# Attention and a quantized MLP on one core: the two score products as pairs of 64-row matmuls, with a ring of three PSUM banks

## The reference

```
x = x + attention(layernorm(x))       # 16 heads of 16 columns
    xw  = x_h @ w_att_val[h]
    att = softmax(xw @ x_h.T / 4)     # [512, 512] per head and batch
    o   = att @ (x @ wv_w.T + wv_b)_h
    attention = o @ out_w.T + out_b
x = x + ffn(layernorm(x))             # blockwise 4-bit quantization, silu(gate) * up, down
```

## Time and profile before

| | |
|---|---|
| median of three runs (lowest, highest) | 1645.03 us (1640.6, 1647.64) |
| profiled execution, first to last instruction | 1643.6 us |
| what the median has beyond that span | 1.4 us |
| attention, about | 66 us to 1075 us |
| MLP | the rest, to 1643.6 us |
| PE busy, DVE busy, ACT busy, POOL busy | 96%, 85%, 51%, 20% |

### The profile page before, as it was taken

One profiled execution on the slowest core, in us unless ns is written; L12 is line 12 of the kernel. 1 busy time (PEld: TensorE's weight loads), 2 busy tenths in 40 slices (PEclk: granted clock), 3 DMA queues, 4 the chain that ended last, 5 costly groups with the idle time before them and its releaser, 6 DMA issues. The chain is left out here.

```text
span 1643.6 us, 30806 instructions
## 1 busy us (share of the span) xinstructions
PE 1573.4 (96%) x7850; PEld 990.7 (60%) x7850; DVE 1397.6 (85%) x2849; ACT 842.4 (51%) x1714; POOL 328.4 (20%) x448
## 2 busy tenths in 40 slices
PE   3499999999999999999999999869999999999998
PEld 3255655655655655655655655446666666666666
DVE  7588888888888888888888887269999999999996
ACT  2166566566566566566566566623333333333332
POOL 2601101101101101101101101023334433344332
PEclk8589999999999999999999999979999999999999
DMA  4735455455455455455455455000000000000000
GB/s 162 154 81 131 93 117 130 92 117 130 92 117 130 92 117 128 93 117 127 94 117 127 94 105 133 3 0 17 16 13 16 16 16 16 13 16 16 16 16 20
DMA packets 67937, 127.28 MB, mean 77 GB/s; under 512 B 22592, under 2 KB 42176, under 8 KB 59456
## 3 DMA queue, kind: packets, MB, share of 16 engines
q1 hardware_dynamic: 60128, 119.53, 33.3%
q10 hardware_dynamic: 7776, 7.36, 2.1%
HBM read 81.67 MB, written 45.15 MB: 77 GB/s over the span
## 5 line engine op out<-in xcount | busy, mean ns | idle before, releaser
L938 DVE TENSOR_REDUCE neg_max<-max_bank 128x1 f32<-128x512 f32 x1024 | 660.4, 683 | 159.0 <-PE max_bank L751 158.1
L880 ACT ACTIVATE probs<-scores 128x512 f32<-128x512 f32 x1024 | 551.2, 599 | 340.8 <-PE scores L759 340.7
L759 PE MATMUL scores<-q_stack,x_stack 98*128 98x512 f32 x1024 | 448.3, 440 | 2.5 <-ACT probs L880 2.0
L751 PE MATMUL max_bank<-x_stack,q_stack 96*128 96x512 f32 x1024 | 413.7, 410 | 16.5 <-DMA x_stack<-x_split 15.1
L759 PEld LDWEIGHTS scores<-q_stack,x_stack 98*128 98x128 f32 x1024 | 193.6, 190 | 245.7 <-ACT probs L880 208.4
L1304 PE MATMUL gu_bank<-splits,f_x_T 128*128 128x352 f32 x1024 | 315.7, 462 | 2.1 <-ACT f_x_T L1282 2.1
L770 PE MATMUL pv<-probs,v_quad 128*32 128x512 f32 x2048 | 272.7, 605 | 0.0
L1304 PEld LDWEIGHTS gu_bank<-splits,f_x_T 128*128 128x128 f32 x1024 | 190.6, 191 | 98.4 <-ACT f_x_T L1282 2.7
L751 PEld LDWEIGHTS max_bank<-x_stack,q_stack 96*128 96x128 f32 x1024 | 198.8, 194 | 53.4 <-issue 15.9
L1322 PE MATMUL y_bank<-splits,h_T 128*128 128x256 f32 x640 | 148.9, 380 | 1.1 <-ACT h_T L1262 1.1
L1262 ACT ACTIVATE h_T<-h_bank 128x512 f32<-128x512 f32 (+1 forms) x128 | 49.0, 434 | 194.5 <-PE h_bank L1314 194.5
(11 more groups left out here) (123 smaller groups left out, 1741.6 us busy)
## 6 DMA issues: line engine op xcount, KB each, us to landing
q_stack<-q_split SPq DMA_DIRECT2D x256, 128.0 KB, 4.0
x_stack<-x_split SPq DMA_DIRECT2D x128, 256.0 KB, 6.0
x_split<-splits SPq DMA_DIRECT2D x64, 256.0 KB, 2.2
q_split<-splits SPq DMA_DIRECT2D x64, 256.0 KB, 2.6
out_dram<-x_all SPq DMA_DIRECT2D x64, 128.0 KB, 1.7
x_all<-in_L_attn_x_dram ACTq DMA_DIRECT2D x14, 512.0 KB, 6.0
max_rows<-max_turned SPq DMA_DIRECT2D x256, 4.0 KB, 4.2
splits<-gate_up_kept SPq DMA_DIRECT2D x1, 1408.0 KB, 5.8
```

The lines of the kernel that those rows point to most:

```text
L751: pe.matmul(max_bank[bank][:, :], q_stack[g][0:KM, h, s * P:(s + 1) * P], x_stack[g][0:KM, h, :], start=True, stop=True).then_inc(m_ready, 1)
L759: pe.matmul(scores[bank][:, :], x_stack[g][0:KS, h, j * P:(j + 1) * P], q_stack[g][0:KS, h, :], start=True, stop=True).then_inc(s_ready, 1)
L880: act.activation(probs[j % 2][:, h, :], scores[bank_of(g, QUAD * j + h)[0]][:, :], ACT.Exp).then_inc(p_ready, 1)
L938: dve.tensor_reduce(neg_max[g % 2][:, TT * h + s:TT * h + s + 1], max_bank[bank_of(g, TT * h + s)[0]][:, :], AX.X, ALU.max, negate=True).t ...
```

## The change

The two products are made by matmuls of 64 contraction rows, in pairs: one on rows 0 to 63 of the array, one on rows 64 to 127, for two different heads and into two different banks (`ROWS = 2`). A stack tile holds four heads as two pairs, so it is half as long. The maximum rows no longer fit into the 64 rows, so each key product gets a second pair of matmuls, accumulated into the same banks, with ones in two of 64 rows against `max_stack`. Key scores have four banks, one for each head. The maximum products and all the other tasks share a ring of three banks, in the order of `TILES_IN_RING`: a tile takes the bank of the tile three before it and waits until that one has been emptied (`room`). `pv` stays a bank of its own; the weighed values of a quad are now summed in two bursts of two steps (in j == 2 for steps 0 and 1, in the next quad's j == 0 for steps 2 and 3), with four tiles of `probs` instead of two.

The other tasks stand at the ends of the odd steps, up to three together. Split work moves: ACT copies x and q out of PSUM whole (`keep`), and POOL makes the high and the low part from SBUF (`split`); POOL also splits the maxima (`split_maxima`) and normalizes (two instructions for a tile of 128 rows). DVE keeps the reduction, the transpose, the statistics and the emptying of `v`, `rows` and `proj`. The maxima's transfers are issued by ACT in j == 0 (one instead of four) and in j == 1 (two instead of one), the latter after a wait for the former. x is stored four times a half instead of twice.

The core of the diff:

```diff
+PAIRS = 2
+ROWS = 2
 BLK = 16
 VW = 32
-KM = 96
-KS = KM + 2
+KM = 4 * D
+STORES = (4 + 2) * 16
...
+    q_stack = [sb(f"q_stack{g}", [P, PAIRS, T], F32R) for g in range(QUADS)]
+    x_stack = [sb(f"x_stack{g}", [P, PAIRS, T], F32R) for g in range(QUADS)]
+    max_stack = [sb(f"max_stack{u}", [P, PAIRS, T], F32R) for u in range(2)]
+    max_ones = sb("max_ones", [P, 1, P], F32R)
...
-    probs = [sb(f"probs{u}", [P, QUAD, T]) for u in range(2)]
+    probs = [sb(f"probs{j}", [P, QUAD, T]) for j in range(TT)]
...
-    scores = [pb(f"scores{k}", [P, T]) for k in range(3)]
-    max_bank = [pb(f"max_bank{k}", [P, T]) for k in range(3)]
+    recip = [sb(f"recip{u}", [P, TT, QUAD]) for u in range(2)]
+    scores = [pb(f"scores{k}", [P, T]) for k in range(QUAD)]
+    ring = [pb(f"ring{k}", [P, T]) for k in range(3)]
     pv = pb("pv", [P, T])
-    misc = pb("misc", [P, T])
...
-    IN_STEP = {(0, 0): "x0", (0, 1): "q0", (0, 2): "rows3", (0, 3): "turn0",
-               (1, 0): "turn1", (1, 1): "proj0", (1, 2): "rows0", (1, 3): "proj1",
-               (2, 0): "x1", (2, 1): "q1", (2, 2): "rows1", (2, 3): "v0",
-               (3, 0): "v1", (3, 2): "rows2"}
...
+    IN_STEP = {(0, 1): ("x0", "rows3"), (0, 3): ("q0", "x1", "turn0"), (1, 1): ("rows0",), (1, 3): ("v0", "turn1"),
+               (2, 1): ("q1", "rows1"), (2, 3): ("proj0",), (3, 1): ("v1",), (3, 3): ("proj1", "rows2")}
...
+    TILES_IN_RING = []
+    for g in range(QUADS):
+        for j in range(TT):
+            TILES_IN_RING += [("max", g, QUAD * j + k) for k in range(QUAD)]
+            TILES_IN_RING += IN_STEP.get((g, j), ())
+    TILES_IN_RING += [None] * (-len(TILES_IN_RING) % len(ring))
+    AT = {tile: n for n, tile in enumerate(TILES_IN_RING) if tile}
+    def bank(tile):
+        return ring[AT[tile] % len(ring)]
...
+    POOL_STEP = {(0, 0): ("maxima", "values0", "x0"), (0, 1): ("values1",), (0, 3): ("values2",),
+                 (1, 0): ("maxima", "q0", "values3"), (1, 1): ("x1",), (2, 0): ("maxima",),
+                 (2, 2): ("deviation",), (2, 3): ("q1",), (3, 0): ("maxima", "normal0"),
+                 (3, 1): ("normal1",), (3, 2): ("normal2",), (3, 3): ("normal3",)}
...
+            def split_maxima(i, g, start):
+                u, n = g % 2, QUAD * TT
+                pool.wait_ge(m_used, n * (i + 1))
+                if not start:
+                    pool.wait_ge(m_turned, i - 1)
+                pool.tensor_tensor(max_cols[u][:, 0:n].bitcast(F32R), neg_max[u][:, :],
+                                   one[:, :].broadcast_to([P, n]), ALU.mult).then_inc(m_split, 1)
+                pool.wait_ge(m_split, i + 1)
+                pool.tensor_tensor(max_cols[u][:, n:2 * n].bitcast(F32R), neg_max[u][:, :],
+                                   max_cols[u][:, 0:n], ALU.subtract).then_inc(m_low, 1)
...
+            def split(kind, b):
+                a = int(kind[1])
+                at, high, low, high_done, low_done = (
+                    (raw[0], xh, xl, xh_done, x_low) if kind[0] == "x" else
+                    (raw[1], qh, ql, qh_done, q_low))
+                pool.wait_ge(kept_used, use(kind, b, BY_ACT) + 1)
+                pool.wait_ge(stored[a], STORES * (b + 1))
+                pool.tensor_tensor(high[:, a, :], at[:, :], one[:, :].broadcast_to([P, T]), ALU.mult).then_inc(high_done, 1)
+                pool.wait_ge(high_done, HALVES * (b + 1) + a + 1)
+                pool.tensor_tensor(low[:, a, :], at[:, :], high[:, a, :].bitcast(F32), ALU.subtract)\
+                    .then_inc(low_done, 1)
...
+            def max_scores(b, g, n):
+                c, q = b + (g + 2) // QUADS, (g + 2) % QUADS
+                p, s = divmod(n, TT)
+                tiles = [("max", g, ROWS * n + m) for m in range(ROWS)]
+                if n == 0:
+                    pe.wait_ge(stack_loaded[q], STACK * (c + 1))
+                for semaphore, count in room(tiles, b):
+                    pe.wait_ge(semaphore, count)
+                for m in range(ROWS):
+                    pe.matmul(bank(tiles[m])[:, :], row_tile(q_stack[q], m)[:, p, s * P:(s + 1) * P],
+                              row_tile(x_stack[q], m)[:, p, :], start=True, stop=True).then_inc(m_ready, 1)
+            def key_scores(i, g, j, p, start):
+                if not (start and j == 0):
+                    pe.wait_ge(p_ready, QUAD * (TT * i + j - 1) + ROWS * p + ROWS)
+                for m in range(ROWS):
+                    pe.matmul(scores[ROWS * p + m][:, :], row_tile(x_stack[g], m)[:, p, j * P:(j + 1) * P],
+                              row_tile(q_stack[g], m)[:, p, :], start=True, stop=False)
+                for m in range(ROWS):
+                    pe.matmul(scores[ROWS * p + m][:, :], row_tile(max_ones, m)[:, 0, :],
+                              row_tile(max_stack[g % 2], m)[:, p, :], start=False, stop=True).then_inc(s_ready, 1)
...
+                for j in steps:
+                    pe.wait_ge(p_ready, QUAD * (TT * i + j + 1))
+                    for k in range(QUAD):
+                        h = head_of(k)
+                        m = pe.matmul(pv[VW * h:VW * h + VW, :], v[q][:, j, h, :], probs[j][:, k, :],
+                                      start=(j == 0), stop=(j == TT - 1))
...
+                    if ahead:
+                        max_scores(b, g, PAIRS * j)
                     if j == 0:
-                        pe.wait_ge(max_loaded[g], 16 * (b + 1))
-                    for h in range(QUAD):
-                        for half in range(2):
-                            if h == MISC_PE[half] and stands(kind, b):
-                                other(half, kind, b)
-                        key_scores(i, g, j, h, start)
-                        if ahead:
-                            max_scores(i + 2, ab, ag, j, (h,), False)
-                    if j > 0:
-                        weigh_values(i, b, g, j - 1, start)
-                    elif not start:
-                        weigh_values(i - 1, b - (g == 0), (g - 1) % QUADS, TT - 1, False)
+                        pe.wait_ge(max_loaded[g], 16 * ROWS * (b + 1))
+                    for p in range(PAIRS):
+                        key_scores(i, g, j, p, start)
+                    if ahead:
+                        max_scores(b, g, PAIRS * j + 1)
+                    if j == 0 and not start:
+                        weigh_values(b, g, True)
+                    if j == 2:
+                        weigh_values(b, g, False)
+                    for kind in IN_STEP.get((g, j), ()):
+                        if stands(kind, b):
+                            other(kind, b)
...
+            def exponentials(i, j, start):
+                for k in range(QUAD):
+                    act.wait_ge(s_ready, QUAD * (TT * i + j) + k + 1)
+                    if k == 0 and j % 2 == 0 and not start:
+                        act.wait_ge(pv_done, 2 * (i - 1) + 1 + j // 2)
+                    act.activation(probs[j][:, k, :], scores[k][:, :], ACT.Exp).then_inc(p_ready, 1)
...
                 for j in range(TT):
-                    exponentials(i, g, j, first and g == 0, range(0, MISC_ACT))
-                    kind = IN_STEP.get((g, j))
-                    if stands(kind, b) and kind[:4] == "turn":
-                        turn(kind, b)
-                    if stands(kind, b) and kind[0] in "xq":
-                        high(kind, b + 1)
-                    exponentials(i, g, j, first and g == 0, range(MISC_ACT, QUAD))
+                    exponentials(i, j, first and g == 0)
                     if j == 0 and not (first and g == 0):
-                        save(i - 1, (g - 1) % QUADS, first)
+                        keep_weighed(i - 1, (g - 1) % QUADS)
+                    for kind in IN_STEP.get((g, j), ()):
+                        if stands(kind, b) and kind[:4] == "turn":
+                            turn(kind, b)
+                        if stands(kind, b) and kind[0] in "xq":
+                            keep(kind, b + 1)
+                    if j == 0 and not (last and g == 3):
+                        store_maxima(i + 1, (g + 1) % QUADS)
+                    if j == 1 and not (last and g == 3):
+                        load_maxima(i + 1, (g + 1) % QUADS)
+            def store_maxima(i, g):
+                act.wait_ge(m_turned, i + 1)
+                act.dma_start(max_rows[bass.ds(i, 1)].rearrange("o c r t -> (o r) c t"), max_turned[g % 2][:, :])\
+                   .then_inc(max_stored, 16)
+            def load_maxima(i, g):
+                act.wait_ge(max_stored, 16 * (i + 1))
...
+                for m in range(ROWS):
+                    act.dma_start(max_stack[g % 2][KM * m:KM * m + 2, :, :].bitcast(F32),
+                                  rows[:, PAIRS * m:PAIRS * m + PAIRS, :]).then_inc(max_loaded[g], 16)
...
+                            reduce_max(i + 2, (g + 2) % QUADS, TT * j + s)
+                        if j == 0 and s == 3 and turning:
```

(64 more changed lines are left out.)

464 lines of the change are left out of this document (209 added, 255 removed).

## The result

The changed kernel is slower by 0.6%: 1655.72 us against 1646.9, medians of five runs each, ratio 1.0059 with a 95% interval of 1.0041 to 1.0077. A second set beside the kernel before gave 1654.44 against 1644.98, ratio 1.0057 (1.0042 to 1.0072). The forecast was slower by 22 us (1645.03 to 1667); it came out slower by 9 (8.8 between the medians of five), under half of that.

What follows compares the result with a forecast made beforehand. PE was taken as the bound. Ring 61.9 plus ACT's 0.5 and 1.1 gave 63.5 us a batch; fifteen batches +25.5, last batch -3, span 1666, median 1667 us. Range 1598 to 1735, the forecast's own 1650 to 1690.

Steps and rivals of the forecast that it cites:

- What a pair costs: On PE, two 64-row matmuls run side by side, one pair taking 0.24 us.
- rival D: Pairs on PE don't run side by side: over 20 us a batch more, 1950; chance 0.10 with its partial form.
- its partial form: Pairs run only partly side by side, 0.31 us each: +5 us a batch, 1740; within the 0.10 of rival D.
- The ring: PE waits nearly 10 us a batch for the three shared banks, eating the pairs' saving: 61.9 us a batch against 61.8.
- Rival A: The ring costs less than half of that worked out: 57.5 to 58.5 us a batch, about 1588; chance 0.28.
- ACT's issues: Issuing the maxima's transfers on ACT delays the copies that (0,1) and (2,1) end on: 0.25 us each, 0.5 a batch.
- ACT's wait for the store: In j == 1 ACT waits for the maxima's store to land, delaying j == 2's exponentials: 1.1 us a batch, bounds 0 and 3.2.
- Rival B: Gains and waits cancel within 0.5 us a batch: 1637 to 1653; chance 0.12.
- Prologue: Before batch 0, still paced by 32 reductions at 0.60 us: change 0.
- Last batch: No maxima after its first half, no preparations, four score banks instead of three: -3 us.
- The q0 chain: q0, moved to (0,3), is split, stored and loaded by near 28.9 us, wanted at about 30: hidden by 1 us.
- C: The stack chain is late at (2,0): 1 to 3 us a batch on top, 1685 to 1715; chance 0.12.

Runs made afterwards that it cites:

- z2: Changed kernel without the second pair of each key product, so exponentials don't subtract the maximum: 1653.85 us against 1654.44.
- y1: Changed kernel with row maxima reduced over 256 of 512 keys, all else kept: 1592.22 us against 1654.44.
- y2: Changed kernel with the first task of each (g, 1) step put in the bank of the weighed values: 1639.94 us, 14.5 less.
- z4: Changed kernel with two stores of the maxima on ACT's queue instead of one: 1675.27 us, 21 more.
- x3: Changed kernel with ACT loading the maxima right behind their store, in j == 0 instead of j == 1: 1806.53 us, 152 more.
- x2: Changed kernel with four stores of the maxima on ACT's queue instead of one: 1776.8 us, 122 more.
- x1: The changed kernel again, unaltered, as the measure for the other runs: 1654.44 us.
- x4: Changed kernel with seven banks instead of three for the maximum products ahead of batch 0: 1648.7 us, 5.7 less.
- y3: Changed kernel with the values weighed in every step instead of two bursts of two: 1638.7 us, 15.7 less.

## Why the prediction was right in sign and wrong in size

**What a pair costs**: 0.24 taken, 0.235 measured. Right; rival D is out, its partial form of 0.31 too. (The estimate of 0.28 that stands beside it, which the sum did not use, was scaled wrongly: by the efficiency that it names it comes to 0.31.)

**The ring**: 61.9 us a batch worked out, 61.99 measured, and step by step close: the even steps 29.4 us together (27.6 + 2.15), the odd ones 32.6 (32.1). The even steps' sum is partly luck, since two errors nearly cancel: from a 64-row pair to the weighing PE takes 0.43, not 0.32, which makes a bare even step 3.56, not 3.45, 0.9 us a batch more; and the late second pairs cost 0.9 us a batch, not 2.15. That the ring is the cause was shown from both sides: 7.5 us a batch less work on PE changes nothing (z2), 0.27 us less in each reduction takes 3.9 us off a batch (y1), and another bank for one task a quad takes 1.0 off (y2). Rival A is out. How much of the wait falls on each single step was not separated.

**ACT's issues, +0.5 us a batch: the step that failed.** "On ACT the first of them stands before the exponentials of j == 1." It does, but it is hidden under the copy of the weighed values: the exponentials are at most 0.05 us late, 0.1 us a batch instead of 0.5, and the loads go out while exponentials or copies run. The path was right: z4's second issue is paid at exactly (0,1) and (2,1), 0.64 and 0.47 us. What failed is that the first one is charged although it overlaps with ACT's computing.

**ACT's wait for the store, +1.1 us a batch: failed too**, and the larger one. I took 3 to 5 us of landing from a row where four stores of the maxima shared SP's queue with the stack loads; one store on ACT's queue has landed after 1.97 to 2.92 us (x3), and the changed kernel's ACT is busy with the exponentials of j == 1 meanwhile; those of j == 2 never wait for it in the steady batches. Why it lands sooner is open: the queue, its neighbours, the number of stores and their size (4 KB, now 16) changed together. x2's four stores on ACT's queue land 1.4 us after the end of the last issue in most quads, but 3.6 to 4.5 in every fourth. Fifteen batches of these two terms are 24 us of the 25.5 forecast; all that a batch is longer by, 0.2 to 0.3 us, makes 3 to 4 us in fifteen. The lower bound that I gave for each, nothing, was nearly the value.

**Rival B** came true for the batch: gains and waits cancel within 0.5 us. The prologue alone lifted the whole out of its range (1637 to 1653).

**Prologue, 0 taken**: wrong by 4.5 us (first key product at 91.45 instead of 86.91; 90.96 in x1), half of the measured loss. "Still paced by 32 reductions" forgot the calculation that the rest of the prediction rests on: two banks of three go to a pair, at the lower clock. x4 gave it back, and 2.5 us more; it is then 3.7 us above the kernel before, which is what the longer batches make.

**Last batch, -3**: from ACT's last load of x (885.52 before, 894.03 after) to the MLP (1083.42, 1091.09) it is 0.8 us less in one profile and 1.6 more in x1's (892.04, 1091.55). This stretch holds the last three batches, so some 0.8 us of it is their longer steady state; what is left for the last batch is nothing that these runs can tell from 0, and not -3.

**The q0 chain** held: one wait for a stack transfer, 0.6 us, between 200 and 1000 us. POOL's split takes 2.3 us (1.04 and 1.28 in its groups) against 2.2; C is out.

The sum with the measured terms, for the two profiles of the changed kernel: prologue 4.5 and 4.1 us, from the first key product to the MLP 3.1 and 4.1, MLP 2.5 and 0. Together 10.2 and 8.1 us, on both sides of the 9 between the medians.

## What to carry to other kernels

Where a faster producer writes into a small ring, work out the ring first: how many tiles the consumer has in hand while the producer waits for two. If that chain already sets the pace, taking work from the producer gives nothing (z2), and a cheaper bank or a better place for the other users of the ring does (y2, y3, x4). Redo the same calculation for the prologue, where clock and latencies differ. And before a step is charged for an issue or a landing, look what the engine is still computing meanwhile and whether the step ends on that engine; a landing from a row with another queue, number or size of transfers is only a bound.

## What the runs showed of the hardware

Two matmuls of 64 rows into different banks cost one start distance, 0.235 us for 512 columns, also with a 128-column weight load each. A transfer's issue on ACT's queue, 0.56 us, is hidden by an ACT instruction already running and blocks the following ones otherwise: a second issue costs 21 us, three more 122, far from in proportion. With four issues, and with the early load (152 us), the granted clock fell to 0.945 and 0.935, from 0.973. In a batch of x3 it falls right behind the stretches in which PE has least to do: PE is busy 1.5 us of the 4 from 594 us and 1.0 of the 4 from 630, and the clock is 0.69 and 0.58 in the 4 us behind each. PE's busy share as such doesn't tell it: z2 has 85% between 200 and 960 us at 1.00, x3's batches 87% at 0.91 to 0.98. The longest single wait of PE differs: 0.6 us in z2 and in the changed kernel, 2.5 in x2, 3.2 in x3. No run varies that alone.
